# A factorization machine on one core: VectorE's last transposition moved ahead, the checks' masks and maxima moved to the end

## The reference

```
xf = x.astype(V.dtype)                    # x: 512 x 6250 int32, V: 6250 x 64 float32
xv = xf @ V
sum_sq = jnp.sum(xv * xv, axis=-1)
sq_sum = xf @ jnp.sum(V * V, axis=-1)
second_order = 0.5 * (sum_sq - sq_sum)
linear = g_bias + xf @ bias
return linear + second_order[:, None]
```

## Time and profile before

| | us |
|---|---|
| median of 3 runs | 49.05 |
| lowest, highest | 49.03, 49.78 |
| the profiled execution | 49.03 |
| its span in the trace | 47.2 |

### The profile page before, as it was taken

How to read it: one execution, slowest core, us unless ns; L and a number is a source line. 1 busy time by engine, 2 the same in 40 slices (tenths; PEclk the granted TensorE clock), 3 DMA queues, 4 the chain that set the end, 5 groups by cost and what they waited for, 6 DMA issues and landing times.

```text
span 47.2 us, 634 instructions
## 1 busy us (share of the span) xinstructions
PE 22.0 (46%) x210; PEld 20.1 (43%) x210; DVE 30.5 (65%) x74; ACT 13.7 (29%) x30; POOL 20.5 (43%) x34
## 2 busy tenths in 40 slices
PE   0000000000000000045999995999999999997200
PEld 0000000000000000045989893998999899985100
DVE  2000000000999469997999899999999999998600
ACT  0000009100899469954996300020002000000000
POOL 1999800000199009999599999990000000000000
PEclk9999999999999999999999999999999999999998
DMA  0399999999999999999999999999999970000000
GB/s 0 102 152 100 109 140 152 164 189 158 175 174 172 181 170 178 146 142 108 105 106 106 106 106 106 101 104 103 116 96 101 94 55 3 0 0 0 0 2 0
DMA packets 5583, 4.87 MB, mean 103 GB/s; under 512 B 1434, under 2 KB 5581, under 8 KB 5581
## 3 DMA queue, kind: packets, MB, share of 16 engines
q0 software_dynamic: 3456, 3.21, 73.4%
q1 hardware_dynamic: 1155, 0.82, 6.7%
q10 hardware_dynamic: 970, 0.81, 5.3%
HBM read 14.48 MB, written 0.00 MB: 307 GB/s over the span
## 4 chain that ended last, share of the span: by engine, by line
DVE 42%; DMA 34%; ACTq 10%; issue 4%; PE 2%; ACT 1%
DMA v_in<-in_L_rec_V_dram 34%; DVE x_all L330 13%; DVE seen L344 13%; ACTq L150 5%; DVE v_rest L295 3%; ACTq L237 3%; DVE xv L354 3%; DVE w_sum L301 2%; DVE xv_sq L359 2%; DVE odd_turned L335 2%; PE xv_ps L466 2%; ACTq L233 2%; DVE seen L406 1%; ACTq L234 1%; DVE seen L350 1%
## 5 line engine op out<-in xcount | busy, mean ns | idle before, releaser
L466 PE MATMUL xv_ps<-wall,x_all 128*128 128x195 bf16 x192 | 19.9, 266 | 1.8 <-DVE x_all L330 1.8
L466 PEld LDWEIGHTS xv_ps<-wall,x_all 128*128 128x128 fp8e4 x192 | 18.0, 105 | 2.7 <-DVE x_all L330 1.1
L160 POOL DMA_DIRECT2D x_all<-in_r_x_dram x24 | 13.0, 551 | 0.8 <-POOLq L498 0.8
L216 POOL TENSOR_TENSOR wall<-v_rest 128x512 bf16<-128x512 f32 (+1 forms) x6 | 7.4, 1247 | 10.2 <-DVE v_rest L295 10.2
L450 PE MATMUL g_ps<-g_in,ones 1*128 1x1 f32 x2 | 0.6, 342 | 20.2 <-DMA g_in<-in_L_rec_g_bias_dram 20.2
L450 PEld LDWEIGHTS g_ps<-g_in,ones 1*128 1x128 f32 x2 | 0.5, 305 | 20.2 <-issue 20.2
L330 DVE STREAM_TRANSPOSE x_all<-x_all 128x512 uint32<-128x512 uint32 (+1 forms) x13 | 8.5, 652 | 0.0
L364 DVE MEMSET v_in<- 22x64 f32 x1 | 0.1, 112 | 10.6 <-DMA v_in<-in_L_rec_V_dram 10.6
L344 DVE TENSOR_TENSOR seen<-seen,x_all 128x512 uint32<-128x512 uint32 (+1 forms) x10 | 6.3, 628 | 0.0
L251 ACT ACTIVATE v_sq<-v_in 128x512 f32<-128x512 f32 (+1 forms) x6 | 3.8, 636 | 5.3 <-DVE v_in L364 3.5
L295 DVE TENSOR_TENSOR v_rest<-v_in 128x512 f32<-128x512 f32 (+1 forms) x6 | 4.3, 750 | 1.4 <-DMA v_in<-in_L_rec_V_dram 1.3
(11 more groups left out here) (27 smaller groups left out, 9.5 us busy)
## 6 DMA issues: line engine op xcount, KB each, us to landing
x_all<-in_r_x_dram POOLq DMA_DIRECT2D x12, 196.0 KB, 9.7
v_in<-in_L_rec_V_dram ACTq DMA_DIRECT2D x6, 128.0 KB, 13.3
v_in<-in_L_rec_V_dram SPq DMA_DIRECT2D x6, 128.0 KB, 11.3
x_all<-in_r_x_dram POOLq DMA_DIRECT2D x4, 100.0 KB, 7.4
x_all<-in_r_x_dram POOLq DMA_DIRECT2D x4, 64.0 KB, 8.5
x_all<-in_r_x_dram POOLq DMA_DIRECT2D x4, 32.0 KB, 8.1
bias_in<-in_L_rec_bias_dram ACTq DMA_DIRECT2D x3, 6.5 KB
v_in<-in_L_rec_V_dram SPq DMA_DIRECT2D x1, 24.0 KB
```

The costliest lines, as they stand in the source:

```text
L160: queue.dma_start(x_words[S * i:S * i + S, t, :, lo // QUAD:hi // QUAD].bitcast(fp8), rows[:, :, START[i] + lo:START[i] + hi]).then_inc(x_ ...
L216: nc.gpsimd.tensor_tensor(placed(n, 2), v_part(v_rest, n), upper(v_rest, n), ALU.subtract).then_inc(low_placed, 1)
L466: last = nc.tensor.matmul(xv_ps[t][:, :, :], rows[:, q, :], wall[:, 1 + QUAD * d + q, :, 0:E], start=(d + q == 0), stop=(d == ND - 1 and q ...
```

## The change

In VectorE's program the last transposition and the third tile's combination change places and both go ahead of the odd check; both masks and both maxima go behind the fourth tile's combination. No instruction is added or removed, and no other engine's program changes.

```
             for u in range(LAST_TURN[T - 2] + 1, last):
                 turn(u)
                 check(u)
+            turn(last)
+            combine(T - 2)
             check_odd(last - 1)
+            combine(T - 1)
             dve.wait_ge(x_seen, last)
             nc.vector.tensor_scalar(seen[:, :], seen[:, :], TOP_BITS, None, ALU.bitwise_and).then_inc(masked, 1)
             dve.wait_ge(masked, 1)
             nc.vector.tensor_reduce(foreign[:, 0:1], seen[:, :], AX.X, ALU.max).then_inc(foreign_ready, 1)
-            combine(T - 2)
-            turn(last)
             nc.vector.tensor_scalar(last_seen[:, :].rearrange("p (g c) -> p g c", g=GT), turn_words(last), TOP_BITS, None,
                                     ALU.bitwise_and).then_inc(masked, 1)
             dve.wait_ge(masked, 2)
             nc.vector.tensor_reduce(foreign[:, 1:2], last_seen[:, :], AX.X, ALU.max).then_inc(foreign_ready, 1)
-            combine(T - 1)
 
             dve.wait_ge(foreign_summed, 2)
```

## The result

| kernel | median, us | lowest, highest | ratio to before | 95% interval |
|---|---|---|---|---|
| before (4 runs) | 49.10 | 49.03, 49.78 | | |
| changed (4 runs) | 49.97 | 49.90, 50.12 | 1.0173 | 1.0128 to 1.0218 |

The change makes the kernel slower by 1.7%; 49.79 was forecast, in a range of 49.36 to 50.08. (Medians here take in all executions; the ratios leave out those that lie over 1.5% above the fastest of the same kernel.) The profiled execution took 50.01 us with a span of 48.2, so 1.8 us lie around the span as before.

What follows compares the result with a forecast made beforehand. Two ends side by side bound the kernel: the output's transfer, deciding, and the flag, with 1.0 us slack at TensorE. Flag 1.74 later, TensorE's drain at 47.74 against 47.0: 49.03 + 0.74 = 49.77, 49.79 against the median; range 49.36 to 50.08.

Steps and rivals of the forecast that it cites:

- The last matmuls start 0.35 sooner: TensorE's last 8 matmuls, freed by the early transposition, start at 42.59 and not at 42.94, a gain of 0.35.
- VectorE's idle time: VectorE before the last combination: idle for 1.8 us, from 41.7 to 43.49.
- The masks and maxima push the flag back by 1.74: Behind VectorE's last combination, masks and maxima delay the flag from 44.59 to 46.33, 1.74 later.
- The handover to an idle TensorE: From the second maximum's end to the weight load of the flag's sum: 0.05 taken, 0.22 as upper end.
- TensorE's branch ends the program: End of program: TensorE, with its branch of 367 ns recurring, drains last at 47.74, 0.74 after the earlier last drain.
- The sum: Whole kernel: 49.03 + 0.74 = 49.77, or 49.79 against the median, 1.5% slower; chance 0.69.
- The slower clock: Rival, chance 0.12: after idling, TensorE computes the flag's sum at its slower clock, adding 0.17 to 0.34; 49.94 to 50.11.
- SyncE last: Rival, chance 0.12: TensorE's branch at the end costs little, so SyncE ends last; +0.37, 49.40.
- The last matmuls no sooner: Rival, chance 0.04: TensorE's last 8 matmuls do not start sooner, so 0.35 is missing from both ends; 50.12.
- the flag covered: Rival, chance 0.03: at the end, the flag stays covered by the output's transfer, so not slower; 48.68.

Runs made afterwards that it cites:

- e3: Changed kernel in which only SyncE loads the flag; the load, branch and general path of ScalarE, VectorE and TensorE are removed; ratio to before 1.0148.
- e9: Changed kernel with SyncE loading the flag and branching first, then waiting for the output's landing; ratio to before 1.0174.
- e11: The changed kernel measured again, unaltered; ratio to before 1.0223.
- e1: Changed kernel with both masks and both maxima ahead of the last combination, in VectorE's idle time; 48.97 us, ratio to before 0.9917.
- e2: As e1, but with the mask and maximum of last_seen behind the last combination; ratio to before 0.9936.
- e10: As e8, but GpSimd instead of SyncE makes the last wait for the output's landing; ratio to before 1.0175.
- e7: Kernel before, with SyncE loading the flag and branching while the output is on its way, waiting for its landing afterwards; 49.30 us, ratio 0.9934.
- e8: e1 with SyncE's order of e7, flag and branch before the wait for the landing; 48.76 us, ratio to before 0.9850.
- e12: e8 with eight increments of an unused semaphore on SyncE behind the wait for the landing; ratio to before 0.9857.

## Why the prediction was right

*The last matmuls start 0.35 sooner.* They do: from the block's start to them 5.36 us (42.77 - 37.41), 5.71 before (42.94 - 37.23). The gap behind L461 is again 0.31. The early transposition waited for no transfer and the third combination for no matmul. VectorE's idle time was 1.95 and not 1.8, because it was done with the odd check 0.16 sooner than summed (4.31 us after the block's start for 4.47).

*The masks and maxima push the flag back by 1.74.* Measured 1.79 (9.15 against 7.36). The spacings are 0.46, 0.60 and 0.32 for a forecast of 0.46, 0.60 and 0.29; the second mask took 0.28 and not 0.25. The handover to an idle TensorE was 0.05 (46.08 to 46.13), the value taken, where the row of before with a busy TensorE showed 0.22.

*TensorE's branch ends the program.* It took 365 ns, and 359 to 368 in the experiments that have it, so it is no accident of one execution, as the prediction held. The reason it took for this is not borne out. The Trainium skill, page "Runtime: NRT & Kernel Launch", section "Instruction fetch mechanics", says that a taken branch outside the fetched pages stalls until a transfer has brought the page. The traces record packets of kind `instruction`, but none in the branch: in the changed kernel none starts between 38.6 us and the end of the span, and the branch starts at 47.5; in the one before none between 38.6 and 47.2, with the branch at 45.5. Unless the transfer is one that the trace does not record, the 365 ns have another cause, which stays open. e3 takes this branch away with the others and gets back 0.3.

*The sum.* Forecast +0.74, the tail grew by 0.8 and the time by 0.87 (49.10 to 49.97). The flag is 0.05 later than summed. TensorE's DRAIN took 71 ns for the 8 ns of the earlier trace rows; it takes 71 or 72 in every other trace in which TensorE loads the flag, so the 8 was the exception. From the flag to that DRAIN it was 0.04 faster (1.36 for 1.40). The last 0.06 between tail and time is within the noise.

*The slower clock* came close and changed nothing. Granted clock of the changed kernel in four stretches, with the columns of the earlier trace rows:

```profile
43.40:46.00 2.60, 0.24 (x3) 0.00 (x1) 2.22 (x7) 0.00 (x0) 0.00 (x0) 1.00 0.03 1
...
46.00:46.20 0.20, 0.07 (x3) 0.07 (x4) 0.08 (x1) 0.00 (x0) 0.00 (x0) 1.00 0.00 0
46.20:46.40 0.20, 0.17 (x4) 0.07 (x4) 0.00 (x0) 0.00 (x0) 0.00 (x0) 0.70 0.00 0
...
46.40:48.20 1.80, 0.00 (x0) 0.00 (x0) 0.15 (x1) 0.00 (x0) 0.00 (x0) 0.50 0.00 0
```

TensorE has nothing to do from 43.6 to 46.13 and is still granted its full 2.4 GHz when the four passes of the flag start. From 46.4 on it has 0.50, which is 1.2 GHz. Between 46.2 and 46.4 the mean is 0.70, so the clock fell at about 46.28 (0.08 us at 1.00 and 0.12 at 0.50 make 0.70). By then 0.15 of the passes' time was over, and they took 0.24, as before. In e9 and e11 they took 0.24 too, and there the granted clock is 1.00 from their start to their end. The rival turned on whether the gap is long enough, and in these three traces it was not. What the passes cost at 1.2 GHz is therefore not measured. The prediction's 0.17 to 0.34 took it from an instruction of another form. The ratio of that form's two times, 0.55 to 0.38, would make 0.35 of the 0.24, which is 0.1 more, an estimate.

*SyncE last* was ruled out by TensorE's branch of 365 ns, but its price was wrong too: +0.37 looked at SyncE and TensorE alone. ScalarE drains 0.1 before TensorE, so with a short branch on TensorE the end would have come, by the drains, 0.1 sooner than it did, where the prediction had 0.37. That the third chain stood so close to the last was not in the prediction, and it did no harm only because TensorE's branch was as long as taken.

*The last matmuls no sooner* and *the flag covered* were the rivals that the drains and the issue of the output rule out; the second of them is what e1 and e2 bring about by another order.

## What to carry to other kernels

Where a program ends in several branches that wait for one flag, the last busy instruction is not the end: read every engine's queue to its drain and write down the slack of each against the last one. Here TensorE had 1.0 us, and no engine's busy time shows it. Work may be moved behind the result's transfer only as far as that slack goes, and idle time in front of the last dependence is the better place for it: with the earlier transposition in both, the kernel loses 0.8 us with the four instructions behind the last combination and gains 0.35 with them ahead of it. A span that gets shorter is not yet a time that does, so compare both.

## What the runs showed of the hardware

- A DRAIN on GpSimd at 47.2 us, long after its last issue of a load, took 2.0 us and ended the program (e10). In the other kernels it starts at 25 to 27 us and takes 14.5 to 15.5, beside the others' work and with no effect on the end.
- Around the span lie 1.8 us in ten kernels; with the span's end moved to 1.8 us behind the output's issue they became 1.9 to 2.5, 2.3 on average (e7, e8). With the end 0.4 later (e12) they were 1.9 on average; whether the time stayed the same is finer than the ratios tell.
- TensorE's branch over the general path took 359 to 368 ns, SyncE's 45 to 50 and ScalarE's 45; but ScalarE's DRAIN starts 0.45 us after its branch does, as late as TensorE's with 0.42. No instruction packet of the trace lies in either stretch.
- Loading the same flag at once, the four engines took 472 (SyncE), 493 (TensorE), 544 (VectorE) and 470 ns (ScalarE) in the changed kernel; in the one before SyncE loaded alone in 473 and the others without it in 488, 546 and 472. They do not hold each other up by more than 5 ns.
